# The low parts of wk, wq and wo in the second attention: made on VectorE in place of GpSimd

## What is computed

```python
xq = (x @ wq).reshape(Bx, Tx, N_HEAD, HEAD_DIM)
xk = (x @ wk).reshape(Bx, Tx, N_KV_HEAD, HEAD_DIM)
xv = (x @ wv).reshape(Bx, Tx, N_KV_HEAD, HEAD_DIM)
xq = xq * cos + _rotate_half(xq) * sin
xk = xk * cos + _rotate_half(xk) * sin
scores = jnp.einsum('bqhd,bkhd->bhqk', xq, repeat(xk)) * scale
probs = jax.nn.softmax(jnp.where(causal, scores, -jnp.inf), axis=-1)
out = jnp.einsum('bhqk,bkhd->bqhd', probs, repeat(xv)).reshape(Bx, Tx, N_HEAD * HEAD_DIM)
x = x + out @ wo
```

## Time and profile before

| | us |
|---|---|
| three runs, median (lowest to highest) | 668.4 (666.92 to 668.41) |
| the profiled execution, device time | 665.93 |
| its span, first to last instruction | 664.1 |
| busy: PE, DVE, ACT, POOL | 581.0, 464.1, 435.5, 458.4 |
| the loop of 64 steps, first p_hi to last lo transpose landed | about 170 to 597 |

### The profile page before, as it was taken

One profiled execution on the slowest core, in us unless ns is written; L12 is line 12 of the kernel. 1 busy time (PEld: TensorE's weight loads), 2 busy tenths in 40 slices (PEclk: granted clock), 3 DMA queues, 4 the chain that ended last, 5 costly groups with the idle time before them and its releaser, 6 DMA issues.

```text
span 664.1 us, 16866 instructions
## 1 busy us (share of the span) xinstructions
PE 581.0 (87%) x7134; PEld 490.3 (74%) x7134; DVE 464.1 (70%) x762; ACT 435.5 (66%) x599; POOL 458.4 (69%) x404
## 2 busy tenths in 40 slices
PE   3888979797888989999999999999999977965796
PEld 2776868786666878888878788888888866854475
DVE  5384556576767877887777777787787765627796
ACT  2232411124889879789788887877987987821694
POOL 7023244442899998998999799799899868742221
PEclk9998989898999999999999999999999999977799
DMA  9050000400699999999999999999999999990001
GB/s 302 16 180 10 0 1 21 83 1 21 108 179 197 193 183 190 196 183 190 181 201 181 201 188 189 192 187 185 198 180 180 182 193 197 195 177 0 1 25 40
DMA packets 317195, 91.79 MB, mean 138 GB/s; under 512 B 305984, under 2 KB 316224, under 8 KB 317120
## 3 DMA queue, kind: packets, MB, share of 16 engines
q1 hardware_dynamic: 316032, 89.67, 77.2%
q10 hardware_dynamic: 1088, 1.05, 0.5%
HBM read 13.11 MB, written 1.05 MB: 21 GB/s over the span
## 4 chain that ended last, share of the span: by engine, by line
PE 38%; DMA 19%; POOL 18%; DVE 11%; ACT 7%; issue 5%; SPq 1%; POOLq 0%; ACTq 0%; DVEq 0%
PE PS L1118 23%; DMA pT_lo<-p_lo 18%; POOL p_lo L487 12%; PE PS L1350 6%; PE PS L1367 4%; DVE small L972 2%; POOL roped L476 2%; ACT p_hi L662 2%; ACT probs L653 2%; PE PS L1371 1%; POOL roped L473 1%; SPq L372 1%; POOL moments L438 1%; DMA pT_hi<-p_hi 1%; DVE stats L748 1%
## 5 line engine op out<-in xcount | busy, mean ns | idle before, releaser
L487 POOL TENSOR_TENSOR p_lo<-probs,p_hi 128x1280 f16<-128x1280 f32 (+7 forms) x128 | 303.8, 2392 | 38.8 <-DMA pT_lo<-p_lo 29.2
L653 ACT ACTIVATE probs<-PS,small 128x640 f32<-128x640 f32 (+7 forms) x256 | 173.7, 742 | 46.1 <-DVE small L972 40.1
L972 DVE TENSOR_REDUCE small<-PS 128x2 f32<-128x1280 f32 (+7 forms) x128 | 172.9, 1351 | 28.7 <-PE PS L1350 27.1
L662 ACT CAST p_hi<-probs 128x1280 f16<-128x1280 f32 (+7 forms) x128 | 145.3, 1159 | 6.9 <-DMA pT_hi<-p_hi 6.1
L1350 PE MATMUL PS<-k_hi,q_hi 64*128 64x512 f32 (+2 forms) x384 | 75.3, 386 | 13.6 <-ACT probs L653 11.0
L1367 PE MATMUL PS<-v_hi,pT_hi 128*128 128x65 f16 x1152 | 79.1, 195 | 1.1 <-DMA pT_hi<-p_hi 0.7
L1371 PE MATMUL PS<-v_lo,pT_hi 128*128 128x64 f16 x1152 | 78.9, 195 | 0.0
L1350 PE MATMUL PS<-k_lo,q_hi 64*128 64x512 f32 (+2 forms) x384 | 78.4, 402 | 0.0
L1367 PEld LDWEIGHTS PS<-v_hi,pT_hi 128*128 128x128 f16 x1152 | 73.6, 99 | 5.0 <-issue 2.8
L1371 PEld LDWEIGHTS PS<-v_lo,pT_hi 128*128 128x128 f16 x1152 | 72.7, 98 | 0.4
L1350 PE MATMUL PS<-k_hi,q_lo 64*128 64x512 f32 (+2 forms) x384 | 67.7, 346 | 0.0
(11 more groups left out here) (190 smaller groups left out, 1431.3 us busy)
## 6 DMA issues: line engine op xcount, KB each, us to landing
wgu_nat<-L_ffn_w_gate_up SPq DMA_DIRECT2D x2, 1024.0 KB, 10.8
wkq_nat<-L_attn_wq SPq DMA_DIRECT2D x8, 256.0 KB, 3.4
wo_nat<-L_attn_wo SPq DMA_DIRECT2D x8, 256.0 KB, 3.3
x<-L_attn_x SPq DMA_DIRECT2D x4, 256.0 KB, 5.3
wdn_nat<-L_ffn_w_down SPq DMA_DIRECT2D x1, 1024.0 KB, 13.1
wfc_nat<-L_ffn_w_fc SPq DMA_DIRECT2D x1, 1024.0 KB, 5.7
wpj_nat<-L_ffn_w_proj SPq DMA_DIRECT2D x1, 1024.0 KB, 8.1
pT_hi<-p_hi SPq DMA_TRANSPOSE x64, 5.8
```

The lines of the kernel that those rows point to most:

```text
L487: nc.gpsimd.tensor_tensor(p16_lo[G % 2][:, cols], probs[G % 2][:, cols], p16_hi[G % 2][:, cols], ALU.subtract).then_inc(p_lo_done, 1)
L653: nc.scalar.activation(probs[G % 2][:, start:start + w], PS[:, src:src + w], ACT.Exp, bias=nmax[:, 4 * (G % 2) + u:4 * (G % 2) + u + 1]).t ...
L662: nc.scalar.copy(p16_hi[G % 2][:, cols], probs[G % 2][:, cols]).then_inc(p_hi_done, 1)
L972: nc.vector.tensor_reduce(nmax[:, first:first + 2], both_heads(part)[:, :, 0:blocks(G, part) * P], AX.X, ALU.max, negate=True).then_inc(nm ...
```

## The change

Six of the eight `split_wkq_low` and all eight `split_wo_low` move from GpSimd's program to VectorE's. The operation, its operands and its semaphores stay as they are. On VectorE they stand right behind `row_max(G, 0)` and before the step's first side job: wo_lo at n = 3, one step later than on GpSimd, wkq_lo at n = 6, one step later too. The last wo_lo stands behind the loop, before the `normalise_o` of step 62. The first two `split_wkq_low`, ahead of the loop, stay on GpSimd.

```diff
@@ gpsimd
-            def split_wo_low(g):
-                pool.wait_ge(wo_hi_done, g + 1)
-                nc.gpsimd.tensor_tensor(wo_lo[:], wo_nat[:], wo_hi[:].bitcast(F32), ALU.subtract).then_inc(wo_split, 1)
...
                 p_low(G, 0)
-                if n == 5 and g + 2 < NG:
-                    split_wkq_low(g + 2)
-                if n == 2 and g:
-                    split_wo_low(g - 1)
-                if G == STEPS - 1:
-                    split_wo_low(NG - 1)
                 p_low(G, 1)
@@ vector
+            def split_wkq_low(g):
+                dve.wait_ge(wkq_hi_done, g + 1)
+                nc.vector.tensor_tensor(wkq_lo[:], wkq_nat[:], wkq_hi[:].bitcast(F32),
+                                        ALU.subtract).then_inc(wkq_split, 1)
+
+            def split_wo_low(g):
+                dve.wait_ge(wo_hi_done, g + 1)
+                nc.vector.tensor_tensor(wo_lo[:], wo_nat[:], wo_hi[:].bitcast(F32), ALU.subtract).then_inc(wo_split, 1)
+
             for G in range(STEPS):
+                g, n, p, r = of_step(G)
                 side(G - 1, 2)
                 row_max(G, 0)
+                if n == 6 and g + 2 < NG:
+                    split_wkq_low(g + 2)
+                if n == 3 and g:
+                    split_wo_low(g - 1)
                 side(G, 0)
...
             for G in range(STEPS, STEPS + PV_LAG):
+                if G == STEPS + 1:
+                    split_wo_low(NG - 1)
                 normalise_o(G - PV_LAG, side_bank(G, "pv"))
```

## The result

The changed kernel is slower: 708.0 us (median of four runs, 706.7 to 708.7) against 667.7 for the kernel before in the same session. The ratio is 1.0605 with a 95% interval from 1.0579 to 1.0632, so +40 us. Forecast were 682 us, +14, and a range up to 691. The direction was right and so was the mechanism that was priced first, but the size was a third of the true one.

The account below looks back on a forecast made before the run. The prediction took TensorE and transpose issue as full, GpSimd a near third. Stalls of 17.3 us less 3.2 and 3.2 cover gave 10.9, moved phases 17.4; taking 14.4 less 0.4 tail, +14 on 668.4: 682 us, range 669 to 691.

Parts of the forecast that it names:

- What bounds the kernel: Second attention's loop: TensorE and transpose issue full, GpSimd a near third; relieving GpSimd returns little more than 4.1 us of gaps.
- The port: Moved operations: a VectorE operation with two SBUF inputs and a GpSimd subtraction exclude each other; the second waits throughout.
- The sign that was named: VectorE's wkq_lo and wo_lo rows: several of 2 to 4.5 us instead of 0.7 to 0.8, mean about 2.
- Who waits: At n = 3 r5 waits for oT_low, at n = 6 wo2 for q_low: VectorE's delay is TensorE's in full.
- the phases: Loop steps: stalls after cover lie between 10.9 us as profiled and 17.4 with shifted arrivals; 14.4 taken.
- The moved case: Once the margin is spent, VectorE arrives 0.6 to 1.9 us into p_lo at n = 3: 17.4 us in all.
- what was written off: Steps 11, 14 and 27 cost 0.2 us together; steps 6, 51, 59 (0.9, 1.4, 3.7) fall where TensorE has time.
- The cover: Loop: 3.2 us of TensorE's waits for pT_lo and a 3.2 us hi transpose margin, spent once, absorb stalls.
- The tail: After the loop: wo_lo no longer stands between the last two p_lo, 0.4 us gained; VectorE's wo_lo is hidden.
- Rival 1: Moved operations' wait short or absent: 0.7 to 0.8 us each place, 7 us covered, about 668 us; chance 0.14.
- Rival 3: Loop and tail faster: transpose issue the one bound, TensorE's stalls inside the margin; -3.5 us, 665; chance 0.08.
- rival 4: GpSimd waits while VectorE works, paying back 0.68 to 0.82 us per operation; 666.5 us; chance within that of Rival 1.

Follow-up runs that it names:

- run 3: The changed kernel with each moved subtraction replaced by an equally long one-SBUF-input reduction in the same place, low parts left out: 666.8 us, ratio 0.9999.
- Run 5: The kernel before plus VectorE reductions over one SBUF tensor behind row_max, 3.7 us at n = 3 and 2.6 at n = 6: 713.5 us, ratio 1.068.
- run 9: The changed kernel with both subtractions on VectorE placed behind oT_low or q_low and normalise_o, before the second row_max: 670.1 us, ratio 1.0042.
- Run 4: The changed kernel with useless matmuls (the filler) on TensorE while it waits for VectorE, 18 at n = 3, 14 at n = 6: 695.4 us, ratio 1.043.
- run 6: The kernel before plus one 1.2 us VectorE reduction over one SBUF input behind row_max at n = 3 and n = 6: 673.1 us, ratio 1.009.
- run 2: The kernel before with only the six wkq_lo of the loop moved to VectorE, wo_lo staying on GpSimd: 684.5 us, ratio 1.025.
- run 8: The kernel before with wo_lo on VectorE at n = 4 and the last in the tail, wkq_lo staying on GpSimd: 675.5 us, ratio 1.011.

## Why the prediction was wrong in size

- **What bounds the kernel.** TensorE is full, as said, and GpSimd third. Of the issue of transposes run 3 shows that it had some room: its gaps over 0.2 us after the first four steps come to 9.6 us there, by the same count 4.3 before, and the time is the same. The gap of 0.33 us in the earlier trace rows is the smallest of the eight (0.33 to 1.15), not of middling size; no sum used it. That the relief would return little fits run 3 (ratio 0.9999), as the net of relief and load.
- **The port.** Right, and by the rows it was read from the earlier trace rows. Run 3 against the changed kernel isolates it. The sign that was named came: wo_lo takes 3.04 us and wkq_lo 2.53 in the mean, where about 2 was forecast. What was left out is that a wait may take in GpSimd's next instructions too (4.47 and 6.48 us).
- **Who waits.** Right: r5 for oT_low and wo2 for q_low, one to one. Run 5 reproduces it without the port, run 9 takes it away.
- **The step that failed first: the price of a stall.** The sum counted an idle us of TensorE as one us. It said nothing of TensorE's clock, which falls to half behind a wait of 2.7 or 3.9 us. Run 4 prices this at some 12 us or more, nearly as much as the whole forecast. Without it the change still costs 29 us, above the range, so a second step must have failed. The rows of before could not show it for this loop, but the page's line of the clock did dip elsewhere (0.969 as a mean over the span), and the prediction did not ask about that.
- **The second: the phases.** "The truth lies between the two, because the first hits are needed to spend the margin: I take 14.4." The first hits came at steps 14 and 19, and from step 19 to step 51 the loop repeats itself to within 0.1 us: wo_lo 3.73 or 3.74 us, wkq_lo 2.67. The moved case, 17.4 us, was the nearer one. Its size at n = 6 was right (2.6 forecast, 2.7 measured). At n = 3 it gave 2.4 to 3.6 and 3.9 was measured, because p_lo starts behind the roped additions, which GpSimd still has, and thus 0.4 us ahead of VectorE.
- **The third: what was written off.** Step 14 was counted at 0.2 us with its neighbours; its wkq_lo took 3.69. VectorE came to it 0.1 us after a p_lo of 3.1 us had begun, where by the rows of before it would have come between two. Steps 51 and 59 were counted as covered; theirs took 3.73 and 1.30. The group of steps 48 to 55 took 57.4 us where it had taken 52.5, so the cover was not there.
- **Together.** TensorE's idle stretches ahead of r5 and wo2 at steps 14 to 46 come to 30.1 us (3.7, four of 3.9, four of 2.7), where the forecast had 17.3, and 23.8 for moved phases. Step 51 adds 3.9. Less the forecast's cover of 6.4 that is 27.6, and the table below gives 28.3 more than before with the filler, without a fall of the clock in these groups, and 43.4 in the changed kernel. By the filler's measure the 15 us between them are the clock's, in these profiled executions; in the times of the runs the filler gives back 12 to 13.

| steps | before, us | changed | with the filler (run 4) |
|---|---|---|---|
| 8 to 15 | 54.6 | 60.2 | 58.6 |
| 16 to 47, four groups, mean | 53.3 | 61.5 | 58.5 |
| 48 to 55 | 52.5 | 57.4 | 55.9 |
| 8 to 55, sum | 320.2 | 363.6 | 348.5 |

- **The cover.** Its sum fits: 6.4 us over five groups are 1.3 a group, and run 6 covers 1.2. That half of it is a margin spent once isn't shown. SyncE had 4.3 us of gaps over 0.2 us after the first four steps, and has 58 in the changed kernel.
- **The tail.** Right: SyncE issues the last transposes back to back (629.95 + 2.73, then 632.72), and the last wo_lo, 3.37 us on VectorE, delays nobody.
- **The rivals.** Rival 1's sum, 668 us, is what run 3 measures once its condition, no wait, holds. Rival 3 fell with it: not even then is there a gain. Of rival 4 a part is there: GpSimd's p_lo take 308.5 us in place of 303.8, so it pays back some 5 of its 19.7 us.

## What to carry over

Before moving an operation between GpSimd and VectorE count its inputs in SBUF: with two of them a VectorE operation waited here for GpSimd's subtractions and additions (3.74 us for 0.68 of work), and the busy shares of the two engines say nothing of that. Then ask what stands behind it in its engine's order. The same operations cost 40 us, with 29 us of waits, ahead of the work that a full TensorE waits for, and 4 us, with 20 us of waits, behind it. And price a stall of TensorE with the clock that it costs: 2.4 us of delay a group cost 1.2 us, and 6.3 cost 8.1.

## What was not expected of the hardware

- An idle stretch of TensorE of 2.7 us was followed by 3.4 us at half its clock (0.50 granted), and so was one of 3.9; with wo_lo alone on VectorE it was 6.8 us behind one of 3.9. In the kernel with 2.3 us of delay the clock fell behind the idle 2.4 us at n = 3 in every group from step 11 to step 51, and behind the 2.3 at n = 6 only once (step 14). In that with 1.2 us it fell at none of these places.
- VectorE and GpSimd do not take strict turns. VectorE came in between two p_lo in the changed kernel (GpSimd's second one took 2.24 us there instead of 1.66), but had to let GpSimd's next instruction pass in run 2 and its next four, 5.8 us of them, in run 8.
- The changed loop runs in one fixed phase: from step 19 to step 46 the waits of group after group differ by 0.01 us, and the four groups take 61.5 us each. Run 3's groups repeat as well (53.5 to 53.6), those of the kernel before don't (52.8 to 54.0 for the same steps). Why is not shown. An average over random arrivals would have been the wrong model here.
